# Selection by batch halves, with the first half inside attention's last steps, and POOL's operations at separate steps

## What is computed

```python
h = tok(x)                                   # 3-level Haar transform, gated bands, inverse
h = h + attn(layernorm(h))                   # 16 heads of 16, causal mask over 256 rows
h = h + ffn(layernorm(h))

def ffn(hs):                                 # hs: [16, 256, 256], 16 experts, capacity 64
    logits = silu(hs @ router_w1) @ router_w2
    probs = softmax(logits.transpose(0, 2, 1), axis=-1)      # over the rows of a batch
    weights, idx = top_k(probs, 64)          # per batch and expert
    weights = weights / (weights.sum(-1, keepdims=True) + 1e-9)
    xin = gather(hs, idx)                    # [16, 16, 64, 256]
    y = (silu(xin @ w1) * (xin @ w2)) @ w3   # per expert
    return scatter_add(idx, y * weights[..., None])
```

## Time and profile before

| | us |
|---|---|
| median of 3 runs (1171.28 to 1172.09) | 1171.4 |
| profiled execution | 1171.56 |
| its span | 1169.8 |

### The profile page before, as it was taken

One profiled execution on the slowest core, in us unless ns is written; L12 is line 12 of the kernel. 1 busy time (PEld: TensorE's weight loads), 2 busy tenths in 40 slices (PEclk: granted clock), 3 DMA queues, 4 the chain that ended last, 5 costly groups with the idle time before them and its releaser, 6 DMA issues.

```text
span 1169.8 us, 19244 instructions
## 1 busy us (share of the span) xinstructions
PE 992.1 (85%) x6998; PEld 826.0 (71%) x6998; DVE 655.2 (56%) x1502; ACT 590.3 (50%) x1105; POOL 732.5 (63%) x658
## 2 busy tenths in 40 slices
PE   0534986989889899886379999999999999999996
PEld 0213465777777777664258888888888888888885
DVE  5866664777777777653733453453453443453441
ACT  0112224777777877785334454454454454454442
POOL 4455434887888888796235665666576575665654
PEclk9778897999999999886679999999999999999999
DMA  8223789778877877601315455445455445455333
GB/s 214 72 72 108 144 188 131 111 140 145 142 142 138 139 145 131 98 30 46 108 55 104 113 104 109 113 86 109 113 104 108 113 86 109 114 104 107 78 55 37
DMA packets 105951, 127.62 MB, mean 109 GB/s; under 512 B 12288, under 2 KB 92160, under 8 KB 104832
## 3 DMA queue, kind: packets, MB, share of 16 engines
q1 hardware_dynamic: 81280, 92.81, 36.4%
q0 software_dynamic: 24576, 33.57, 17.7%
HBM read 79.67 MB, written 46.14 MB: 108 GB/s over the span
## 4 chain that ended last, share of the span: by engine, by line
PE 49%; DVE 2%; POOL 1%; issue 1%; DMA 0%; ACT 0%; POOLq 0%; ACTq 0%
PE y_ps L1172 16%; PE gate_ps L1158 15%; PE value_ps L1158 15%; PE xT_ps L1139 2%; DVE top_index L1312 1%; DVE top L1306 1%; DVE work L1314 0%; PE gate_ps L1181 0%; POOL out L1114 0%; POOL x_rows L1103 0%; DMA x_rows<-normed_scratch,slot_row 0%; DMA rw2s<-in_L_ffn_router_w 0%; ACT xg_hi L1205 0%; DVE L L1304 0%; DVE rw_shifted L1296 0%
## 5 line engine op out<-in xcount | busy, mean ns | idle before, releaser
L1114 POOL DMA_INDIRECT out<-y_rows,slot_row x128 | 202.9, 1585 | 192.2 <-ACT y_rows L1218 163.0
L249 POOL TENSOR_TENSOR probs_k<-probs_full,probs_k 128x512 f16<-128x512 f32 x192 | 223.1, 1170 | 66.9 <-ACT probs_k L650 66.6
L1281 DVE TENSOR_TENSOR hidden<-silu_g,value_ps 128x512 f32<-128x512 f32 x128 | 88.1, 688 | 306.2 <-PE value_ps L1158 171.4
L1226 ACT ACTIVATE silu_g<-gate_ps 128x512 f32<-128x512 f32 x128 | 76.6, 598 | 276.6 <-PE gate_ps L1158 276.6
L1103 POOL DMA_INDIRECT x_rows<-normed_scratch,slot_row x128 | 146.9, 1148 | 56.3 <-issue 38.7
L643 ACT ACTIVATE probs_full<-scoresT_ps,log 128x512 f32<-128x512 f32 x192 | 131.8, 687 | 87.3 <-PE scoresT_ps L474 55.8
L1172 PE MATMUL y_ps<-w_hi,hidden_lo 128*128 128x256 f32 x512 | 144.9, 283 | 0.0
L1172 PE MATMUL y_ps<-w_lo,hidden_hi 128*128 128x256 f32 x512 | 144.9, 283 | 0.0
L1172 PE MATMUL y_ps<-w_hi,hidden_hi 128*128 128x256 f32 x512 | 144.7, 283 | 0.0
L650 ACT ACTIVATE probs_k<-probs_full 128x512 f16<-128x512 f32 x192 | 119.7, 624 | 0.0
L1158 PE MATMUL gate_ps<-xg_hi,w_hi 128*128 128x512 f32 x256 | 103.4, 404 | 2.1 <-ACT xg_hi L1205 2.1
(11 more groups left out here) (206 smaller groups left out, 2333.3 us busy)
## 6 DMA issues: line engine op xcount, KB each, us to landing
w_raw<-in_L_ffn_w SPq DMA_DIRECT2D x48, 512.0 KB, 4.1
q_stack<-q_scratch SPq DMA_DIRECT2D x96, 128.0 KB, 4.8
k_stack<-k_scratch SPq DMA_DIRECT2D x96, 128.0 KB, 7.6
x_tile<-in_x SPq DMA_DIRECT2D x4, 1024.0 KB, 5.0
h_scratch<-rec_tile SPq DMA_DIRECT2D x4, 1024.0 KB, 3.9
hacc<-h_scratch SPq DMA_DIRECT2D x4, 1024.0 KB, 5.4
q_scratch<-q_hi SPq DMA_DIRECT2D x16, 256.0 KB, 2.2
q_scratch<-q_lo SPq DMA_DIRECT2D x16, 256.0 KB, 2.5
```

The costliest lines, as they stand in the source:

```text
L249: G.tensor_tensor(probs(b, 1, n), pf[N % 3][:].rearrange("p (a q) -> p a q", a=4 if n % 3 == 2 else 2), probs(b, 0, n), ALU.subtract).then ...
L1114: G.indirect_dma_start(out=rows, out_offset=bass.IndirectOffsetOnAxis(ap=idx[:, col:col + 1], axis=0), in_=ys[c][:, j, :], in_offset=None, ...
L1226: A.activation(sg[ft % 2][:], GP[ft % 2][:], ACT.Silu).then_inc(silu_done, 1)
L1281: V.tensor_tensor(hf[ft % 2][:], sg[ft % 2][:], VP[ft % 2][:], ALU.mult).then_inc(hf_done, 1)
```

## The change

Slots are divided by batches: half 0 is batches 0 to 7, half 1 batches 8 to 15. A unit is an expert and a half, with 64 slots of two batches on the partitions of each of four columns. The tiles of the selection, the raw tiles of the expert weights, expert 0's weight parts and the first gathered rows are allocated ahead of `front`, on memory that earlier steps of `front` have ceased to use.

Within `front`'s steps: the SiLU of batches 0 to 7 at step 150 (ACT), the load of the second router weights at 181 (SP), their shifted copies at 182 to 190 (now POOL), the load of expert 0's weights at 186, logits of half 0 at 193 to 196 (PE), its 24 selection operations at 197 to 216 (DVE), expert 0's high parts at 215 to 217 (ACT) and low parts at 220, 225 and 231 (now DVE), the turned lists at 218, the first gather at 225 (POOL), SiLU and logits of batches 8 to 14 at 219 to 230, the slot weights of half 0 at 229 to 233.

In `experts` the order of the first units is (expert 0, half 0), (1, 0), (0, 1), (1, 1), then by expert. The selection of half 1 runs on DVE ahead of unit 0 (3 rounds) and inside it (5 rounds); its lists and weights are turned within unit 1. Expert 1's low parts are POOL's; expert 2's weights are split at the end of unit 3.

In attention's steps: `LN1` goes from -30 to -36, so the first steps are 6 more (`CUT` keeps its two values); both powers come ahead of `probs_lo` in their step; `v_rest` moves from `VP_ + 4` to `VP_ + 6`, the second subtraction from `VP_ + 7` to `VP_ + 10`, ACT's part between them by two steps; the first product of the second LayerNorm and all behind it come one step later.

```diff
-    LN1, XT, QP, KP, VP_, EX, MT, LN2, HT, RT = -30, -21, -18, -16, -12, 22, 13, 42, 53, 58
+    LN1, XT, QP, KP, VP_, EX, MT, LN2, HT, RT = -36, -21, -18, -16, -12, 22, 13, 42, 53, 58
-    CUT = (FIRST + 12, FIRST + 24)
+    CUT = (-18, -6)
+        SILU, LOAD, SHIFT, RAW, LOGITS, TOP = 150, 181, 182, 186, 193, 197
...
# POOL's steps
+                    if t == 225:
+                        g.wait_ge(idx_done, 2)
...
+                        for j in range(4):
+                            G.indirect_dma_start(out=sel.xr0[:, j, :], out_offset=None, in_=hn_dram[0:8 * S],
...
+                    if t == SHIFT:
+                        g.wait_ge(st_ps, NB * 13)
+                        G.memset(sel.rw2p[:], 0.0).then_inc(rw2_done, 1)
+                        for i in range(2):
+                            G.iota(sel.base[64 * i:64 * i + 64], pattern=[[8 * S, 2], [2 * S, 4], [0, E]], base=i * S, channel_multiplier=0,
...
+                    if 0 < t - SHIFT <= 8:
+                        i = t - SHIFT - 1
+                        G.tensor_copy(sel.rw2p[:, i, i * E:(i + 1) * E], sel.rw2s[:]).then_inc(rw2_done, 1)
+                        g.wait_ge(rw2_done, 2 + i)
...
-                    b, r = due(t, VP_ + 4)
+                    b, r = due(t, VP_ + 6)
                     if r == 0:
                         g.wait_ge(v_hi, b + 1)
...
-                    if r == 3:
+                    if r == 4:
                         g.wait_ge(v_mid, b + 1)
# PE's steps
+                    if 0 <= t - LOGITS < 4:
+                        n = t - LOGITS
+                        pe.wait_ge(hid_done, n + 1)
...
+                    if t == LISTS + 1:
+                        pe.wait_ge(lists_done, 1)
+                        pe.transpose(SR[1][:, 0:P], sel.ixf[:, 0].rearrange("p i s -> p (i s)"), ident[:]).then_inc(pos_ps, 1)
+                    if 221 <= t < 224:
+                        n = t - 221
+                        pe.wait_ge(hid_done, 5 + n)
...
+                    if t == 230:
+                        pe.wait_ge(hid_done, 8)
+                        pe.matmul(SR[0][:, 0:S], sel.rw2p[:, 6], rh[:, 14 * S:15 * S], start=False, stop=True).then_inc(lg_ps, 1)
+                    if t == 232:
+                        pe.wait_ge(w_done, 1)
...
# ACT's steps
+                    if t == SILU:
+                        act.wait_ge(rh_done, 8)
+                        for n in range(4):
+                            A.activation(rh[:, 512 * n:512 * (n + 1)], rh[:, 512 * n:512 * (n + 1)], ACT.Silu).then_inc(hid_done, 1)
+                    if 215 <= t < 218:
+                        m = t - 215
+                        act.wait_ge(w0_in[m], 16)
...
+                        A.activation(sel.W0[m][0][:], sel.raw[m][:], ACT.Copy).then_inc(w0_hi, 1)
+                    if t == LISTS + 1:
+                        act.wait_ge(lists_done, 1)
+                        A.activation(sel.ex[:], sel.L[0][:], ACT.Exp, bias=sel.nm[:, 0:1], accum_out=sel.Z[:, 0:1]).then_inc(ex_done, 1)
...
# DVE's steps
+                    if t == TOP:
+                        v.wait_ge(lg_ps, 1)
+                        tp.step(V.tensor_copy(sel.L[0][:], SR[0][:, 0:S]))
+                    for i in range(3 * ROUNDS):
+                        if t == TOP + i * 5 // 6:
+                            top_step(tp, V, sel, 0, i, ROUNDS)
...
+                    for m in range(3):
+                        if t == (220, 225, 231)[m]:
+                            v.wait_ge(w0_hi, m + 1)
+                            V.tensor_tensor(sel.W0[m][1][:], sel.raw[m][:], sel.W0[m][0][:].bitcast(F32), ALU.subtract).then_inc(w0_lo, 1)
+                    if t == 229:
+                        v.wait_ge(ex_done, 1)
+                        v.wait_ge(et_done, 1)
+                        top_weights(tp, V, sel, 0, w_done)
...
# experts
+    SEQ = [(0, 0), (1, 0), (0, 1), (1, 1)] + [(e, c) for e in range(2, E) for c in range(2)]
...
+                    if U == 1 and ft == 1:
+                        pe.wait_ge(w_done, 1)
+                        pe.transpose(XP[1][:, 0:P], sel.wt[:, 1].rearrange("p i s -> p (i s)"), ident[:]).then_inc(w_ps, 1)
-                    if ft == 1 and U + 1 < NU:
+                    if ft == (3 if U == 1 else 1) and U + 1 < NU:
                         turn(U + 1)
...
+                if U == 0:
+                    act.wait_ge(lists_done, 1)
+                    A.activation(sel.ex[:], sel.L[1][:], ACT.Exp, bias=sel.nm[:, 1:2], accum_out=sel.Z[:, 1:2]).then_inc(ex_done, 1)
```

More of the change, by code:

```diff
@@ new lines, with selection_tiles @@
+class Selection:
+    pass
+def selection_tiles(sb, S, E, CAP):
+    s = Selection()
+    s.rw2s = sb("rw2s", [P, E])
+    s.rw2p = sb("rw2_shifted", [P, 8, P])
+    s.L = [sb(f"logits{r}", [P, S]) for r in range(2)]
+    s.wk = [sb(f"work{r}", [P, S]) for r in range(2)]
+    s.top = sb("top", [P, 2, CAP])
+    s.ix = sb("top_index", [P, 2, CAP], U32)
+    s.ixf = sb("top_index_f", [P, 2, 2, CAP])
+    s.nm = sb("neg_max", [P, 2])
+    s.ex = sb("ex", [P, S])
+    s.et = sb("ex_top", [P, 2, CAP])
+    s.wt = sb("top_weight", [P, 2, 2, CAP])
+    s.Z = sb("Z", [P, 2])
+    s.tot = sb("tot", [P, 2])
+    s.base = sb("row_base", [P, 2, 4, E])
+    s.idx = sb("slot_row", [P, 2, 4, E], U32)
+    s.ws = sb("slot_weight", [P, 2, 4, E])
+    return s
@@ new lines, in top_step @@
+def top_step(c, V, sel, r, i, rounds):
+    k, part = divmod(i, 3)
+    src = (sel.wk if k else sel.L)[r]
+    new = sel.top[:, r, 8 * k:8 * k + 8]
+    if part < 2:
+        c.wait()
+    if part == 0:
+        c.step(V.max(new, src[:]))
+    elif part == 1:
+        if k == 0:
+            c.step(V.tensor_scalar(sel.nm[:, r:r + 1], sel.top[:, r, 0:1], -1.0, None, ALU.mult))
+        c.step(V.max_index(sel.ix[:, r, 8 * k:8 * k + 8], new, src[:]))
+    elif k < rounds - 1:
+        c.step(V.match_replace(sel.wk[r][:], new, src[:], BIG))
@@ new lines, in top_round, with slot_rows, slot_weights @@
+def top_round(c, V, sel, r, k, rounds):
+    for part in range(3):
+        top_step(c, V, sel, r, 3 * k + part, rounds)
+def slot_rows(V, sel, r, pos, done):
+    for i in range(2):
+        h = slice(64 * i, 64 * i + 64)
+        V.tensor_tensor(sel.idx[h, r], pos[h].rearrange("p (j i e) -> p j i e", j=4, i=2)[:, :, i], sel.base[h, r], ALU.add).then_inc(done, 1)
+def slot_weights(V, sel, r, turned, done):
+    for i in range(2):
+        h = slice(64 * i, 64 * i + 64)
+        V.tensor_copy(sel.ws[h, r], turned[h].rearrange("p (j i e) -> p j i e", j=4, i=2)[:, :, i]).then_inc(done, 1)
@@ L417, in _ @@
             sp.wait_ge(hn_out, 16 * B)
+            for j in range(4):
+                sp.wait_ge(rows0_in[j], 16)
         @block.tensor
@@ L1025, in experts @@
         ps = lambda n, s, d=F32: ctx.enter_context(nc.psum_tensor(n, s, d))
[L1027 to L1045, removed]
+        sb("early_room", [P, 14112])
+        raw = sel.raw
+        W = [sel.W0, [[sb(f"w{m + 1}_{x}1", [P, 1024], F32R) for x in ("hi", "lo")] for m in range(3)]]
+        xr = [sel.xr0, sb("x_rows1", [P, ST, D])]
         xg = [[sb(f"xg_{x}{i}", [P, KT, N], F32R) for x in ("hi", "lo")] for i in range(2)]
@@ L1131, in turn @@
             def turn(U):
-                e, c = U // 2, U % 2
                 if U:
@@ L1337, in _ @@
+                for en, m in splits(U):
+                    if en > 1:
+                        weight_lo(en, m)
             for kt in range(KT):
                 x_lo(0, kt)
+            v.wait_ge(lg_ps, 1)
+            c1.step(V.tensor_tensor(sel.L[1][:], sel.L[1][:], YP[0][:, 0, :], ALU.add))
+            for k in range(HEAD):
+                top_round(c1, V, sel, 1, k, ROUNDS)
             for U in range(NU):
```

330 lines of the change are left out of this document (186 added, 144 removed).

## The result

| | us |
|---|---|
| before, median of 4 runs (1171.28 to 1172.09) | 1171.61 |
| after, median of 4 runs (1136.77 to 1141.65) | 1138.57 |
| ratio | 0.9726, 95% interval 0.9709 to 0.9742 |
| profiled execution after, its span | 1141.65, 1139.9 |

The change takes 33 us off, where 38 were forecast; by the profiled executions it is 29.9 (spans 1169.8 and 1139.9), because the one of after is the slowest of its four.

A forecast was written before the change was run, and what follows sets the result against it. It saw PE bounding the expert units, 41 us of unhidden selection and 2.7 us of PE idle per attention cycle. Terms (a) to (h) summed to -38.2 from 1171.56, forecast 1133 us, range 1121 to 1146.

The forecast's parts named there:

- (g): Between the two blocks, last router copy to first gate matmul: 41.15 us falls to 4.7, -36.4.
- (e): Steps 193 to 217: logits and selection fit beside attention but stand ahead of `rden`, +2.0, bounds 0 and 5.
- (f): Tail to the last router copy: turned weights, DVE weight halves and logits lengthen the chain, +3.9, bounds 0 and 6.
- (h): First expert units: second half's selection, lists, table changes and gather cost +2.5, bounds 0 and 8.
- (a): Ten attention cycles: spreading POOL's extra work takes each from 22.94 to 21.90 us, -10.4 in all.
- first rival: Attention cycles keep 22.94 us because DVE's normalisation at step 7 is stretched beside POOL; 1143 us, chance 0.15.
- (b): Start: first LayerNorm six steps earlier lets DVE begin tile 3 at about 115.2 instead of 118.6, -3.4.
- (c): Step 150's cycle: four SiLUs and two table loads, 4.7 us on ACT, partly covered by POOL's idle 2.7, +2.0.
- (d): Steps 182 to 190: shifted router weights put about 3.6 us on POOL, which has 2.0 idle, +1.6.
- Units 4 to 31 are as before: Later expert units: unchanged at 17.55 us each, PE without a gap.

The follow-up runs named there:

- e1: Changed kernel with DVE's LayerNorm product as scalar_tensor_tensor, reciprocal deviation in PSUM as a second input, instead of tensor_scalar: 1133.13 us, ratio 0.9691.
- e6: Kernel before with the change's attention part alone, plus the LayerNorm product in e1's form: 1155.12 us, ratio 0.9875.
- e8: e1's kernel with e4's later low halves, second SiLU batch at 223, its logits at 227 to 229, slot weights at 225: 1130.99 us, ratio 0.9662.
- e5: Kernel before with the change's attention part alone, selection and experts as before: 1162.45 us, ratio 0.993.
- e4: Changed kernel with DVE's three low halves of expert 0's weights moved to steps 231, 234 and 235: 1138.86 us, ratio 0.9734.
- e11: Changed kernel run once more, unaltered, with another profile: 1142.44 us, ratio 0.9745.
- e2: Changed kernel with expert-block tiles behind the early ones moved up by 896 bytes per partition: 1138.15 us, ratio 0.9724.

## Why the prediction was right and where not

The sign, the size within the range and the source were right: the gain is (g), and the selection did fit beside attention. The forecast's own mechanism for the cycles was wrong. That the sum came out no further off is in part luck: (e), (f) and (h) were too high by 5.1 together in the profiled execution, against the 7.6 that (a) lost.

(a) is the step that failed, by 7.6 us. It took a cycle without a first LayerNorm as the measured form of the new cycle, with the sentence that `rden`'s wait hangs on what the change doesn't touch. But that cycle has no normalisation at step 7. The first rival had the mechanism, the rows and nearly the price: 2.46 against 0.74 is 1.7 us of DVE for the two instructions, where it said up to 1.9. It placed the new wait on `row_max`; it came on `rden`, 0.7 long. I gave it 0.15 because DVE idles over 5 us a cycle; that is no argument where one operation stands directly ahead of a reciprocal for which PE waits. e1 and e6 show the cause: with another form of that operation the new wait is gone, and the cycles come down to 21.9, some to 22.0 to 22.7. The Trainium skill (SBUF — State Buffer, "Who interferes with whom") also says that a DVE instruction with at most one input in SBUF and outside the two-port modes does not contend, and that one with two inputs in SBUF does with a GpSimd one that reads it; the 0.86 of e1's form and the 2.18 of the residual sum beside `w_lo` agree.

(b) was right in mechanism: tile 3 starts on DVE at 115.53 (about 115 forecast, 118.59 before), and the first exponentials are 2.9 earlier.

(c) was near at 2.6, but for a cycle of 22.74. In the cycle of 21.88, for which it was worked out, it is 3.7 (at clock 0.93): a cover of 2.7 by POOL's idle time was too large. Part of the 3.7 may be the clock's; in e8 the same cycle takes 27.13, at 0.92. The table loads took 1.28 each with a SiLU 0.01 behind, as in the earlier trace rows.

(d) was near at the clock that it assumed (1.1 against 1.6), but the 1.1 is made of two: the shifted weights and what came with them add 2.4 to the 16.49 of the attention part alone, which is itself 1.3 below the cycle before. The profiled 3.3 is the 1.1 and some 2 us that go with a lower clock, which no term had.

(e) was too high: the selection's operations cost nothing; DVE has 21.54 us of work in 33.61, and without the selection these steps take 33.78 and 33.68 (e5, e6). In (f) the size was too high (2.6 for 3.9), and what I added up was not the chain: in e4 POOL's operations are short again and nothing is gained, and in e8 the tail is 2.0 shorter. The order in which PE stands behind the SiLUs, of which I had priced 0.6 for the products only, explains both; it was not changed by itself, so it is not shown alone.

(g) was right within 0.3, though the 5.08 are made otherwise: 1.9 is the gap at the end of the block, put down to the gather's rows, which I had taken to run beside the tail.

(h) was too high for the first units (0.6) in the profiled execution. Unit 1 takes 18.40, not 20, and unit 0 ran at a clock of 1.00 where it had run at 0.86. In e11, the same kernel, unit 0 took 2.2 more at 0.89, and the term would be 2.9, so its size hangs on the clock. Unit 0 before, and in e11:

```profile
595.38:615.60 20.22, 20.22 (x105) 17.57 (x105) 8.63 (x12) 7.82 (x13) 4.14 (x5) 0.86 0.17 43
562.42:584.11 21.69, 20.52 (x105) 17.39 (x106) 18.41 (x51) 9.68 (x14) 6.36 (x4) 0.89 0.22 80
```

"Units 4 to 31 are as before" was wrong: 2.4 us, from the placement of the weights (e2).

## What to carry to other kernels

Moving an operation to an emptier step is not enough; look at what runs beside it on the other engine there, and at who is queued behind it. Before a cycle of the old trace is taken as the model of the new one, list what the new one has and it has not. When a stall is removed and nothing is gained, a wait of the same engine on the next instruction is the first place to look.

## What was not expected of the hardware

Even experts' units took 17.72 against 17.55 with the same instructions and PE without a gap, by the place of the weights towards the other tiles alone. And cycles with much waiting ran at different granted clocks in different executions of the same instructions: 18.86 us at 1.00, 21.15 at 0.84. The cycle behind the first maxima took 23.96 to 27.33 at 0.74 to 0.81, and not in the order of the clock (26.32 at 0.81), so there it is not the clock alone. The changed kernel's runs spread by 0.6%, where the prediction took 0.2% for what can be told from no change; a term under 2 us in those stretches can't be told from this.
